# Writing out a two-turn loop on five engines in a graph-network kernel

## What is computed

```python
for i in range(NUM_BLOCKS):            # 4 blocks
    y = _cond_layer_norm(x, cond, s1_w[i], s1_b[i], b1_w[i], b1_b[i])
    y = _sparse_attention(y, src, dst, wq[i], bq[i], wk[i], bk[i], wv[i], bv[i], wo[i], bo[i])
    x = x + y
    y = _cond_layer_norm(x, cond, s2_w[i], s2_b[i], b2_w[i], b2_b[i])
    y = jax.nn.relu(y @ m_w1[i] + m_b1[i]) @ m_w2[i] + m_b2[i]
    x = x + y
```

## Time and profile before

| | before |
|---|---|
| median of 3 runs | 886.33 us (883.48 to 887.07) |
| profiled execution, its own time | 891.0 us |
| its span, first to last instruction | 889.3 us |
| mean granted TensorE clock | 0.985 of full |
| PE busy | 839.7 us, 94% |
| DVE busy | 560.2 us, 63% |
| ACT busy | 398.0 us, 45% |
| POOL busy | 231.4 us, 26% |

### The profile page before, as it was taken

One profiled execution on the slowest core, in us unless ns is written; L12 is line 12 of the kernel. 1 busy time (PEld: TensorE's weight loads), 2 busy tenths in 40 slices (PEclk: granted clock), 3 DMA queues, 4 the chain that ended last, 5 costly groups with the idle time before them and its releaser, 6 DMA issues. The chain is left out here.

```text
span 889.3 us, 13979 instructions
## 1 busy us (share of the span) xinstructions
PE 839.7 (94%) x4222; PEld 636.4 (72%) x4223; DVE 560.2 (63%) x1221; ACT 398.0 (45%) x646; POOL 231.4 (26%) x253
## 2 busy tenths in 40 slices
PE   4999789999889999999997999999999998999998
PEld 2666557667677778777695777787786965688786
DVE  5999987748957666576656476664776664730110
ACT  3999893325345612355322365223563233531210
POOL 5000023207422124402235122234013414412200
PEclk9999999999999999999999999999999998999999
DMA  7999914715525653636541546436477377220100
GB/s 167 192 214 241 275 39 124 188 58 133 154 59 123 179 125 107 147 102 178 122 136 54 140 98 183 100 106 146 102 193 176 115 192 184 56 96 0 48 13 35
DMA packets 37846, 113.39 MB, mean 128 GB/s; under 512 B 5908, under 2 KB 6472, under 8 KB 30108
## 3 DMA queue, kind: packets, MB, share of 16 engines
q1 hardware_dynamic: 20604, 79.00, 37.5%
q10 hardware_dynamic: 17184, 33.69, 11.3%
HBM read 105.33 MB, written 7.34 MB: 127 GB/s over the span
## 5 line engine op out<-in xcount | busy, mean ns | idle before, releaser
L690 POOL TENSOR_TENSOR wl<-wraw,wh 128x512 fp32r<-128x512 f32 x140 | 179.7, 1318 | 395.3 <-ACT wh L768 361.7
L1806 PE MATMUL ring<-ohs,ohd 128*128 128x512 f32 x312 | 80.2, 410 | 6.4 <-DVE ohs L1317 6.4
L1806 PEld LDWEIGHTS ring<-ohs,ohd 128*128 128x128 f32 x312 | 59.2, 195 | 31.5 <-issue 18.6
L1295 DVE SCALAR_TENSOR_TENSOR ohd<-iota,dstT,vals 128x256 fp32r x156 | 69.9, 481 | 9.2 <-PE ring L1806 5.6
L768 ACT ACTIVATE wh<-wraw 128x2048 fp32r<-128x2048 f32 x35 | 66.8, 1909 | 9.4 <-DMA wraw<-in_L_gnn_root 4.7
L793 ACT ACTIVATE yT_h<-ring 128x512 fp32r<-128x512 f32 x32 | 19.0, 598 | 98.7 <-PE ring L1722 98.7
L817 ACT ACTIVATE ohs<-iota,minus_srcT 128x512 fp32r<-128x512 f32 x78 | 52.4, 713 | 17.4 <-PE ring L1806 11.1
L1733 PE MATMUL mix_ps<-quad,att_shift 120*32 120x512 f32 x384 | 52.0, 622 | 3.7 <-DMA quad<-in_L_gnn_basis 3.7
L695 POOL TENSOR_TENSOR rstd<-ve,half 128x1 f32<-128x1 f32 x44 | 24.2, 553 | 111.9 <-DVE ve L1146 111.6
L1704 PE MATMUL ring<-yT_h,wh 128*128 128x512 f32 x128 | 49.8, 389 | 0.0
L1704 PE MATMUL ring<-yT_l,wh 128*128 128x512 f32 x128 | 49.8, 389 | 0.0
(11 more groups left out here) (390 smaller groups left out, 2157.4 us busy)
## 6 DMA issues: line engine op xcount, KB each, us to landing
quad<-in_L_gnn_basis SPq DMA_DIRECT2D x60, 960.0 KB, 8.2
wraw<-in_L_gnn_m_w ACTq DMA_DIRECT2D x8, 1024.0 KB, 6.0
mix_scratch<-mixed SPq DMA_DIRECT2D x128, 32.0 KB, 3.9
wraw<-in_L_gnn_wv ACTq DMA_DIRECT2D x4, 1024.0 KB, 5.3
wraw<-in_L_gnn_wq ACTq DMA_DIRECT2D x4, 1024.0 KB, 5.1
wraw<-in_L_gnn_wk ACTq DMA_DIRECT2D x4, 1024.0 KB, 5.3
wraw<-in_L_gnn_wo ACTq DMA_DIRECT2D x4, 1024.0 KB, 5.4
wraw<-mix_scratch ACTq DMA_DIRECT2D x4, 1024.0 KB, 5.7
```

Of the source, the lines that this page charges most:

```text
L690: last = g.tensor_tensor(wl[s][:, k, :], wraw[s][:, k, :], wh[s][:, k, :].bitcast(F32), ALU.subtract)
L1295: return v.scalar_tensor_tensor(out, at.unsqueeze(1).broadcast_to([P, 4, HALF]), dstT[:, e], vals[:, e, :].rearrange("p a b -> p (a b)").u ...
L1806: last = te.matmul(ring[:, banks[b], :], ohd[:, s, b, :], ohs[:, s, :], start=False, stop=False)
```

## The change

The loops over the middle blocks become Python loops, so the blocks' instructions are written once for each turn, with constants in place of the register. Nothing else changes; the instructions that do work and their order are the same on each engine.

```diff
@@ -599,7 +599,7 @@
             block_loads(0, 1, False)
-            with sp.Fori(1, BLOCKS - 1) as i:
+            for i in range(1, BLOCKS - 1):
                 block_loads(i, i + 1, False)
@@ -741,7 +741,7 @@
-            with pool.Fori(0, BLOCKS - 1) as i:
+            for i in range(BLOCKS - 1):
                 block_lows(i, False)
             block_lows(BLOCKS - 1, True)
@@ -1042,7 +1042,7 @@
             block_highs(0, False, True)
-            with act.Fori(1, BLOCKS - 1) as i:
+            for i in range(1, BLOCKS - 1):
                 block_highs(i, False)
             block_highs(BLOCKS - 1, True)
@@ -1627,7 +1627,7 @@
             attention_block(0, False, True)
-            with dve.Fori(1, BLOCKS - 1) as i:
+            for i in range(1, BLOCKS - 1):
                 attention_block(i, False)
             attention_block(BLOCKS - 1, True)
@@ -2124,7 +2124,7 @@
             attention_block(0, False, 2)
-            with pe.Fori(1, BLOCKS - 1) as i:
+            for i in range(1, BLOCKS - 1):
                 attention_block(i, False)
             attention_block(BLOCKS - 1, True)
```

## The result

The kernel after takes 874.3 us (median of 4 runs, 873.81 to 876.72), the kernel before on the same chip 885.57 us; the ratio is 0.986 with an interval of 0.983 to 0.988. A second comparison (e2) gave 874.07 against 888.29, ratio 0.985 (0.983 to 0.987). The profiled execution took 874.51 us with a span of 873.0, against a span of 889.3 before.

The account below looks back on a forecast made before the run. PE, busy 94% of the span, bounds the kernel; only its stops and low clock can be won. DVE's branch (-6.99) and register instructions (-1.15) give -8.14 us: 886.33 becomes 878.2 us, range 874.5 to 883.5.

Parts of the forecast that it names:

- The branch back on DVE (-6.99): Start of block 2: without DVE's branch its head falls from 85.19 to 78.20 us, including PE's 5.20 us stop.
- the stall stays: Rival: something else at this place in the second turn causes the 5.76 us; only tails gain, 885.2 us; chance 0.06.
- Why DVE alone: At the branch into block 2, DVE's 280-row body isn't held and is fetched again while `wk` loads; 5.76 us gap.
- The register instructions (-1.15): Layer norm in the tails of blocks 1 and 2: constants save 0.57 and 0.58 us; nothing in the heads.
- The branch back on PE, ACT, POOL and SP (nothing): Loop turns of these engines: PE's body is held, POOL and ACT in time, SP's loads not waited for; zero gain.
- So I carry the 8.1 over as they are: The blocks' gain from the profiled execution, 891.0 us, is taken unchanged off the median: 886.33 - 8.14 = 878.2 us.
- The sum itself: Whole kernel: DVE's branch and the tails' register instructions together, -6.99 - 1.15 = -8.14 us.
- That can't save time, so its lower end is nothing: Added code, 354 more PE rows and five more code packets in block 2: no gain, cost taken as nothing.
- The gain wasn't lost later: Rival: a longer `quad` wait in the third layer eats the gain, 886.3 us; chance 0.04 for all, 0.05 for part.
- No code came late: Rival: late fetches in straight code, 7 us each; one gives 885.2 (chance 0.04), two or more 892.2 us (0.03).
- The range's lower end: Lower limit of the forecast time, 874.5 us: 875 from the runs' 3.6 us spread, with a little room below.

Follow-up runs that it names:

- e2: The kernel after, unchanged, measured once more against the kernel before: 874.07 against 888.29 us, ratio 0.985 (0.983 to 0.987).
- e3: The kernel before with DVE's loop alone written out: 879.5 us, ratio 0.990 (0.987 to 0.992).
- e4: The kernel before with all loops but DVE's written out: 884.19 against 888.29 us, ratio 0.995 (0.993 to 0.996).
- e10: The kernel before with DVE's loop written out but the block number kept in a register, so register instructions stay: ratio 0.992 (0.990 to 0.994).
- e11: The kernel before with 240 drains (instructions without work) added to POOL's loop body, 288 instructions in all: ratio 1.000 (0.998 to 1.003).
- e16: The kernel before with 128 drains added to ACT's loop body, 305 instructions in all: one run, 888.90 us.
- e17: The kernel before with DVE's loop written out and 128 drains in ACT's kept loop body, 305 instructions: ratio 0.990 (0.987 to 0.993).
- e5 to e8: The kernel before with one engine's loop written out in each, SP, POOL, ACT and PE in turn: ratios 0.999, 0.998, 1.000 and 0.998.
- e14: The kernel before with 37 drains behind the last instruction of POOL's program, all loops kept: ratio 0.998 (0.996 to 1.001).
- e15: The kernel after with 203 drains behind the last instruction of POOL's program: ratio to the kernel before 0.990 (0.986 to 0.993).
- e18: The kernel before with DVE's loop written out and 37 drains behind POOL's last instruction, POOL's loop kept: ratio 0.987 (0.984 to 0.989).
- e8: The kernel before with PE's loop alone written out: ratio 0.998 (0.996 to 1.001).

## Why the prediction was right and where it was not

**The branch back on DVE (-6.99): right.** The head of block 2 changed by -6.99, the "issue" row of 5.76 us and PE's 5.20 us are gone. e3 and e4 show that it is DVE's loop, e10 that it is the branch and not the register instructions. The rival "the stall stays" is refuted by the same row. The trace puts the stop on the branch itself: in the kernel before, DVE's next instruction behind it, a register instruction that waits for no semaphore, begins 5.71 us after the branch.

**Why DVE alone: the explanation given is not confirmed.** "A body that isn't held whole has to be read again from its start" took 300 instructions as too long and 177 as short enough. POOL with 288 and ACT with 305 turned with 0.27 and 0.28 us between the branch and the next instruction (e11, e16, e17). In these bodies 240 and 128 of the instructions are drains. The Trainium skill ("Runtime: NRT & Kernel Launch", section "Instruction fetch mechanics") gives the window as 512 instructions for these engines. By that figure the bodies of 288 and 305 would turn freely, as they do, but so would DVE's of 300, which stands for 5.6 to 6.3 us in each of the 11 profiles that keep its branch, with two or three packets on q14 in that gap.

It isn't that DVE turns any loop slowly: in the set-up it turns a loop of 164 instructions (L1340, eight turns), and its next instruction begins within 0.4 us after each branch there, in every profile. Nor does the load of `wk` fill the transfer engines through the whole stop. The two packets of the earlier trace rows start at 476.2 and 479.8 us, and from 480 us until DVE goes on at 481.89 the engines are idle:

```profile
479.00:480.00 1.00, 0.00 (x0) 0.00 (x0) 0.00 (x0) 0.00 (x0) 1.00 (x2) 1.00 0.69 264
480.00:481.00 1.00, 0.00 (x0) 0.00 (x0) 0.00 (x0) 0.00 (x0) 1.00 (x2) 1.00 0.00 0
```

So contention with that load can account for a part at most. Where the body lies in memory, or what else DVE's code does, may decide; this wasn't tried, and why DVE alone stops stays open.

**The register instructions (-1.15): right.** The two tails gave -1.13, the blocks of e10 against those of after 1.05.

**The branch back on PE, ACT, POOL and SP (nothing): right for the turn, wrong for the program.** e5 to e8 leave the blocks unchanged. But the step looked only at the place of the loop. POOL's program got longer, and with that alone the start changed. Over the 20 profiles of the table, 12 have a share of 0.17 to 0.29 from 7.6 to 10.6 us and 8 have 0.88 to 1.02, none between. In the first group POOL's built program has 226, 466 or 475 instructions, in the second 263, 272 or 306. Block 0's mark comes at 316.2 us on average in the first and 313.0 in the second, so about 3.2 us of the profile's 4.18 are this (single profiles overlap: 313.75 in e11, 314.47 in e18). That POOL's code alone switches it, without any change ahead of its last instruction, is shown by e14, e15 and e18. The programs of the other engines did not switch it where they alone changed, not even PE's with 548 instructions more (e8). Why is open: the lengths don't order the groups in one direction, and what is placed behind POOL's code in memory can't be seen in a trace.

**"So I carry the 8.1 over as they are": the step that failed.** The sum itself met the blocks within 0.05 us (-8.14 against -8.09). What it lacked is a term for the rest of the program. The prediction put that at nothing or at a cost: of the added code it says "That can't save time, so its lower end is nothing", and POOL's loop it cost at nothing. In the profiles the longer code of POOL took about 3.2 us from the start (2.4 us in the timed means above). Perhaps there is also a gain at the end: the stretch from block 3's mark on was 4.02 us shorter in the first pair of profiles, 1.5 of them PE's wait for `quad` and 2.6 behind it, where PE's clock averaged 1.00 and not 0.98. Over all profiles this stretch takes 207.3 to 211.0 us with DVE written out and 208.8 to 212.3 with its loop, means 208.8 and 210.2. PE's wait for `quad` varies with no engine to tie it to (1.8 to 4.0 us). In this profile it was short and PE's clock stayed whole after it, against the earlier trace rows; in e2 the wait was the same 2.26 us and the eight products behind it took 1.94 us again:

```profile
730.56 1.06 PE L1733 MATMUL mix_ps<-quad,att_shift 120*32 120x512 f32 x8 [2.26 <-DMA quad<-in_L_gnn_basis]
```

Blocks 8.1, start about 3.2 and end about 1.3 make 12.6 us; the medians of the two comparisons lie 11.3 and 14.2 us apart. How much of the last term is chance isn't settled, nor why e4, with DVE's loop kept, gained 4.1 us where POOL alone gained 1.4. That 874.3 lies only 0.2 us below the range is no credit to the sum: the room below 878.2 was for the spread of the runs, not for these terms.

**The rivals.** The gain wasn't lost later: the `quad` wait came 13.7 us earlier and was shorter. No code came late: no "issue" gap of over 1 us is left on any engine in the blocks, those on DVE in the set-up are in the kernel before as well, and PE's five additional packets cost nothing seen in the windows. The range's lower end, from the spread of the runs alone, allowed for no other part of the program to get faster; that is where it was too narrow.

## What to carry to other kernels

Where a loop's turns stand beside written-out copies of the same block, cut both at the same marks and compare: the two terms read in that way came out within 0.02 us each. Write out one engine's loop at a time: here DVE alone brought the whole gain of the blocks, and the other engines went on within 0.35 us of their branches back. And a longer program of one engine can move the first 20 us, even if that engine isn't busy: here POOL's did, and those of DVE, ACT and PE did not. Before a difference of a few microseconds is put down to an edit, compare the starts, and pad the program behind its last instruction to see how much is the layout.

## What was not expected of the hardware

- The transfers at the start have two modes that depend on the built program and not on the loads: from 7.6 to 10.6 us the transfer engines' share is 0.17 to 0.29 or 0.88 to 1.02, the 17 us from the start hold 2.59 MB in before against 3.08 in after, and POOL's four instructions behind them take 3.81 against 1.99 us. 37 drains behind POOL's program switch it (e14).
- POOL with a loop body of 288 instructions and ACT with 305 go on 0.27 and 0.28 us after their branches back, while DVE with 300 stands for 5.6 to 6.3 us.
- The 5.2 us for which PE waits then are followed by a stretch at the low clock that differs between executions: 0.74 to 0.87 of the full clock in the next 13 us.
- A wait count held in a register costs DVE's chain little but not nothing: about 0.5 us in each tail, none in the heads.
